# Gated cross-attention block: order of the tiled runs, place of the turned maxima and order of ScalarE's work in the attention steps

## The reference, cut to what matters

```
x (16, 100, 512), ctx (16, 361, 512), 16 query heads, 4 key heads, head size 32
Q = layernorm(x) @ Wq ; K = ctx @ Wk ; V = ctx @ Wv            # per batch entry
scores = Q K^T / sqrt(32) + slope * (key - query), masked
w = softmax(scores) ; out = (w V) @ Wo ; x = x + tanh(g0) * out
h = silu(q(ln(x)) q(Wg)) * (q(ln(x)) q(Wu)) ; h = rms_norm(h) ; x = x + tanh(g1) * q(h) q(Wd)
```

## Time and profile before

| what | value |
|---|---|
| median of three runs | 549.12 us |
| profiled execution, its span | 552.41 us, 550.6 us |
| TensorE busy | 485.2 us, 88% |
| VectorE busy | 363.5 us, 66% |
| ScalarE busy | 335.2 us, 61% |
| GpSimd busy | 236.8 us, 43% |
| chain that ended last, by engine | PE 66%, DVE 10%, DMA 9%, ACT 8%, issue 5% |

### The profile page before, as it was taken

How to read it: one execution, slowest core, us unless ns; L and a number is a source line. 1 busy time by engine, 2 the same in 40 slices (tenths; PEclk the granted TensorE clock), 3 DMA queues, 4 the chain that set the end, 5 groups by cost and what they waited for, 6 DMA issues and landing times.

```text
span 550.6 us, 8360 instructions
## 1 busy us (share of the span) xinstructions
PE 485.2 (88%) x2881; PEld 304.3 (55%) x2898; DVE 363.5 (66%) x672; ACT 335.2 (61%) x565; POOL 236.8 (43%) x253
## 2 busy tenths in 40 slices
PE   0699979997989989997999998589999999999964
PEld 0699979997944444443444444245455555555421
DVE  3786644386456777784988874166777777777750
ACT  0466646484246666765656676447777777777661
POOL 1000000000066767574264720066667676776650
PEclk9999989999989999998999999879999999999997
DMA  7879896999258897786676702002333333333222
GB/s 179 264 216 412 321 376 206 292 333 270 90 125 201 189 188 202 164 219 147 126 172 161 195 2 98 0 1 39 77 79 76 76 76 76 76 78 76 68 58 48
DMA packets 55666, 83.28 MB, mean 151 GB/s; under 512 B 30770, under 2 KB 42242, under 8 KB 53710
## 3 DMA queue, kind: packets, MB, share of 16 engines
q1 hardware_dynamic: 50446, 57.64, 40.9%
q0 software_dynamic: 3456, 12.58, 8.6%
q10 hardware_dynamic: 1728, 12.58, 6.5%
HBM read 57.29 MB, written 9.85 MB: 122 GB/s over the span
## 4 chain that ended last, share of the span: by engine, by line
PE 66%; DVE 10%; DMA 9%; ACT 8%; issue 5%; SPq 1%; POOL 0%; POOLq 0%; ACTq 0%; DVEq 0%
PE wide L1302 12%; PE bank L1136 10%; PE bank L1177 7%; PE bank L1312 7%; PE bank L1229 7%; PE bank L1219 6%; PE wide L1205 6%; PE bank L1232 5%; PE wide L1136 5%; DMA ct<-ctx_t 4%; ACT p_t L679 3%; DVE row_max L935 3%; DMA qs<-nm_t 2%; DMA wq_f<-wq 2%; ACT xq_f L718 1%
## 5 line engine op out<-in xcount | busy, mean ns | idle before, releaser
L935 DVE TENSOR_REDUCE row_max<-wide 100x2 f32<-100x722 f32 x128 | 110.4, 902 | 38.8 <-PE wide L1205 38.7
L679 ACT ACTIVATE p_t<-bank 121x400 f32<-121x400 f32 x192 | 92.5, 504 | 52.7 <-PE bank L1219 49.0
L1302 PE MATMUL wide<-w_q,xq 128*128 128x512 bf16 (+1 forms) x403 | 94.1, 384 | 1.6 <-ACT xq L726 0.8
L543 POOL TENSOR_TENSOR z<-h,lnw 128x512 f32<-128x512 f32 (+1 forms) x52 | 66.6, 1281 | 34.3 <-DVE h L1044 26.6
L1302 PEld LDWEIGHTS wide<-w_q,xq 128*128 128x128 bf16 (+1 forms) x416 | 40.1, 100 | 51.7 <-issue 6.6
L1312 PE MATMUL bank<-w_q,yq 128*128 128x512 bf16 (+1 forms) x204 | 51.0, 394 | 9.7 <-DMA yq<-y_int 9.2
L499 POOL DMA_DIRECT2D quant_in<-w_ffn x24 | 14.3, 597 | 101.3 <-PE bank L1177 94.8
L1205 PE MATMUL wide<-ks,qs 101*100 101x362 f32 x192 | 49.6, 346 | 9.4 <-DVE row_max L935 5.2
L774 ACT ACTIVATE act<-wide,small 128x512 f32<-128x512 f32 (+1 forms) x52 | 35.1, 680 | 35.3 <-PE wide L1302 23.4
L1219 PE MATMUL bank<-qs,ks 103*121 103x400 f32 x144 | 50.6, 381 | 6.4 <-DMA qs<-nm_t 3.1
L1177 PE MATMUL bank<-wv_f,ct 128*121 128x128 f32 x384 | 48.7, 288 | 3.3 <-DMA ct<-ctx_t 3.3
(11 more groups left out here) (139 smaller groups left out, 913.3 us busy)
## 6 DMA issues: line engine op xcount, KB each, us to landing
quant_in<-w_ffn POOLq DMA_DIRECT2D x24, 512.0 KB, 6.0
ct<-ctx_t SPq DMA_DIRECT2D x16, 722.0 KB, 9.9
ks<-k_all SPq DMA_DIRECT2D x36, 181.0 KB
q_scratch<-qhl SPq DMA_DIRECT2D x16, 400.0 KB, 8.1
abs_a<-w_ffn ACTq DMA_DIRECT2D x6, 1024.0 KB, 7.3
abs_b<-w_ffn ACTq DMA_DIRECT2D x6, 1024.0 KB, 8.9
qs<-q_scratch SPq DMA_DIRECT2D x12, 400.0 KB
xb<-x SPq DMA_DIRECT2D x12, 256.0 KB, 2.8
```

What stands on the lines that cost most here:

```text
L543: nc.gpsimd.tensor_tensor(z[par][0:rows, c], h[0:rows, c], lnw[0:rows, c], ALU.mult).then_inc(z_done, 1)
L679: nc.scalar.activation(p_t[:, j, :], bank[j % 2][0:KT, 0:HQ], ACT.Exp).then_inc(exp_done, 1)
L935: nc.vector.tensor_reduce(row_max[b % 2][:, 2 * u:2 * u + 2], wide[u % 2][0:SQ, :, 0:SK], AX_X, ALU.max).then_inc(s_maxed, 1)
L1302: mm = nc.tensor.matmul(wide[j % 2][0:rows, m, :], xq[:, c, 0:rows], w_q[:, m * C + c, 512 * j:512 * j + 512], start=(c == 0), stop=(c == ...
```

## The change

The table of what stands behind each pair of scores is new, so that PV0 and PV1 follow each other without anything between them. The transposed maxima go to columns 400 to 499 of bank 3 from entry 1 on. ScalarE does `turned_max` and e6, e7 before `log_sums` and `inverse_sums` of the older entry, and `keep_pv` after e'1 where it was after e'2. The wait of `scores(b, 1)` for `nm_ready` stays for b = 1 alone; PV0 waits for `nm_ready` instead, and the transposition waits for the copies of the step before.

```diff
-BEHIND = {0: [("t", 2, 4), ("t", 2, 5), ("pv", 2, 0), ("turn", 1, 0), ("t", 2, 6), ("t", 2, 7)],
-          1: [("t", 2, 8)],
-          2: [("t", 2, 9), ("t", 2, 10)],
-          3: [("t", 2, 11), ("pv", 2, 1)],
-          4: [("t", 1, 0)],
-          5: [("t", 1, 1), ("t", 1, 2), ("pv", 2, 2)],
-          6: [("t", 1, 3)],
-          7: []}
+BEHIND = {0: [("t", 2, 4), ("t", 2, 5), ("turn", 1, 0)],
+          1: [("t", 2, 6), ("t", 2, 7)],
+          2: [("t", 2, 8), ("t", 2, 9)],
+          3: [("pv", 2, 0), ("pv", 2, 1)],
+          4: [("t", 2, 10), ("t", 2, 11)],
+          5: [("t", 1, 0), ("t", 1, 1)],
+          6: [("pv", 2, 2), ("t", 1, 2)],
+          7: [("t", 1, 3)]}
...
+        def turned(b):
+            return wide[1][0:2 * H, 0, 400:400 + SQ] if b == 0 else bank[3][0:2 * H, 400:400 + SQ]
...
-                copy_high(nm_t[:, :], wide[1][0:2 * H, 0, 400:400 + SQ]).then_inc(nm_ready, 1)
+                copy_high(nm_t[:, :], turned(b)).then_inc(nm_ready, 1)
...
             def attention_step(b):
                 if b >= 2:
                     exps(b - 2, 4, 5)
-                if b >= 3:
+                if 2 <= b <= B:
+                    turned_max(b - 1)
+                if b == B + 1:
                     log_sums(b - 3)
                     inverse_sums(b - 3)
-                if 2 <= b <= B:
-                    turned_max(b - 1)
                 if b == B + 1:
                     xq_round(0)
                 if b >= 2:
                     exps(b - 2, 6, 7)
                 if b == B + 1:
                     xq_out(0)
+                if 3 <= b <= B:
+                    log_sums(b - 3)
+                    inverse_sums(b - 3)
                 if b >= 2:
                     exps(b - 2, 8, 9, 10, 11)
                 if b <= B:
-                    exps(b - 1, 0, 1, 2)
+                    exps(b - 1, 0, 1)
                 if b >= 2:
                     keep_pv(b - 2)
                 if b <= B:
-                    exps(b - 1, 3)
+                    exps(b - 1, 2, 3)
...
-                if b > 0 and u == 1:
-                    pe.wait_ge(nm_ready, b)
+                if b == 1 and u == 1:
+                    pe.wait_ge(nm_ready, 1)
...
+                if kt == 0:
+                    pe.wait_ge(nm_ready, min(b + 2, B))
...
             def turn_maxima(b):
                 pe.wait_ge(nm_split, b * 2 + 2)
-                nc.tensor.transpose(wide[1][0:2 * H, 0, 400:400 + SQ], nm_q[:, :].bitcast(F32), ident[0:SQ, 0:SQ]).then_inc(nm_turned, 1)
+                if b >= 2:
+                    pe.wait_ge(o_copied, (b - 1) * 2)
+                nc.tensor.transpose(turned(b), nm_q[:, :].bitcast(F32), ident[0:SQ, 0:SQ]).then_inc(nm_turned, 1)
```

## The result

Four runs of the changed kernel gave 565.91 us in the median (561.28 to 568.23), against 550.10 us for the kernel before (four runs, 547.73 to 552.56). The ratio is 1.0255, with an interval of 1.0201 to 1.031: 2.6% slower. The forecast was 551.6, in a range of 546.0 to 556.5, so the time lies outside it. The profiled execution took 568.23 us with a span of 566.4 us, 15.8 more than the one before.

A forecast was written before the change was run, and what follows sets the result against it. A woven chain, mostly on TensorE with short waits, was taken to bound the 11.65 us step. Terms -3.2 - 1.2 + 1.55 + 1.1 + 1.1 + 1.4 + 0.3 + 1.4 = +2.45 took 549.1 to 551.6 us, range 546.0 to 556.5.

The forecast's parts named there:

- The step itself: Undisturbed attention step, laid out from old distances: 11.42 us against 11.65, so -3.2 over fourteen steps.
- Step 9: t'0 waits for the stored maxima behind wo_f's load, issued 2.3 later in its step: +1.55.
- Step 16: The output product of 2.77 stands ahead of t6 and starves ScalarE: +1.4.
- The two new waits: PV0 waits for the maxima's copy, the transposition for keep_pv: both said to cost nothing.
- Step 2: PV run escapes the clock's lower level, as ScalarE paces that stretch: -1.2, or +1.4 if the clock is still low.
- VectorE has split the maxima by 1.13: In the laid-out step, row_max 7 and two operations of 0.2 end at 1.13, the transposition follows at 1.22.
- VectorE is later nowhere: Scores 6, at 8.58 in the laid-out step, need row_max 4, done at 8.08.
- In an undisturbed step I cost this at nothing: Stored maxima queued behind the later load on SyncE's queue: cover nearly gone, yet no cost in undisturbed steps.
- a cover between +0.25 and -0.85: Maxima wanted by t'0 at 8.15 in the step, forecast to land at 7.9 to 9.0.
- The first rival: Stored maxima wait behind the load in every step: +4.0 on the forecast, 555.6 us; chance 0.22.
- the forecast's own 2.65: DMA terms for late maxima: +1.55 in step 9 and +1.1 in steps 3 and 4.
- two one-off terms: wo_h holds ScalarE 1.90 before the fourth exponential: +1.1; wo_l holds VectorE 2.20 before row_max 0: +1.4.

The follow-up runs named there:

- e1: Changed kernel with the load of queries and keys cut to some 1/30 of the bytes from entry 4 on: 565.04 us, ratio 1.0273.
- e12: Changed kernel with the maxima's transposition behind t7, their store on ScalarE's queue, and wo_f's load and splits three steps later: 562.09 us.
- e13: Changed kernel with loads of the weights GpSimd quantises cut to 16 columns from the third block on, its operations whole: 561.64 us, ratio 1.0174.
- e7: Changed kernel with GpSimd's weight operations cut to 16 columns and the small load of queries and keys: 552.32 us, ratio 1.0007.
- e6: Kernel before the change with GpSimd's weight operations cut to 16 columns: 564.87 us, ratio 1.0259.
- e10: Changed kernel with the maxima's store issued by ScalarE on its own queue from entry 2 on: 589.17 us, ratio 1.0719.
- e4: Changed kernel with t10 and t11 ahead of the merged run, and ScalarE's logarithm and inverse behind four exponentials: 565.25 us, ratio 1.0315.

## Why the prediction was wrong

**Right.** The step itself, 11.43 where 11.42 was laid out, with the handovers of the earlier trace rows. Step 9: t'0 waited 3.86 where 2.73 + 1.55 was laid out. Step 16 and what follows: +2.3 where +1.4 stood, the same way though larger. The two new waits for banks (PV0 for the copy, the transposition for `keep_pv`) cost nothing, as said.

**Right in number only.** Step 2: scores 0 to scores 6 took 10.0 (157.04 to 167.07) against 11.6, so -1.6 where -1.2 stood. But an undisturbed step of the new order takes 8.7 for it (291.10 to 299.83), where the old one took 10.0, so step 2 is still 1.3 over its own order, with the granted clock at 0.50 until 162.7, where it was 1.6 over. The relief is 0.3; the rest comes of the new order reaching scores 6 earlier in every step. That the number fitted was luck.

**The first failed step** is "The two new waits cost nothing", in its last part: "VectorE has split the maxima by 1.13" and "VectorE is later nowhere". That left the transposition, at 1.22, a cover of 0.09. Before, a whole run of tiled matmuls stood between the earlier trace rows. I took the split's two operations as 0.2 each from an undisturbed step, and never asked what they last when GpSimd is at its weights, though the earlier trace rows show it there. Held, one of its operations takes 0.4 to 1.05 here and up to 1.3 in e1. Scores 1 and t6 stand behind the transposition in TensorE's order, so the wait holds them too. The sum had no term for this; it measured 5.0 in three steps.

**The second** is "In an undisturbed step I cost this at nothing", said of a cover between +0.25 and -0.85. An expected loss whose bounds reach to -0.85 in each of fourteen steps is not nothing. The first rival was this mechanism, and the alternation is its two-step loop. Its price of 4.0 on top of the forecast's own 2.65 is 6.65; 5.4 was measured. Its reason (the store cannot pass the load on one queue) is not enough after e12 and e13: it is the traffic of load and weights together.

**The third** is the size of two one-off terms. `wo_h` and `wo_l` stood at +1.1 and +1.4 over the kernel before. In e7, where nothing else is in the way, the two steps cost 8.1 us over undisturbed ones, against 1.1 in e6; in the changed kernel it is 8.0 against 1.2, with one held split in it: 6.8 where 2.5 stood. The waits were foreseen, the slower matmuls behind them were not.

With these three the account closes: for the thirteen steps the forecast had -3.0 + 2.65 + 2.5 = +2.15; 2.75 more for landings, 5.0 for held splits and 4.3 for `wo_f`'s splits make 14.2, and 14.1 was measured.

**Behind all three** stands an absent term: the clock. Working out -1.2 in step 2 I used the fall of the earlier trace rows, but costed no wait elsewhere at what it does to TensorE. Rows of the chain in the changed kernel, the merged run of step 11, behind a wait of 1.87 for VectorE that `wo_l` makes:

```profile
281.64 1.49 PE bank L1238 x8
...
283.12 1.33 PE bank L1241 x8
...
284.46 1.30 PE bank L1238 x8
...
285.75 0.67 PE bank L1241 x8
```

From 281.64 to scores 4 at 286.43 it takes 4.79 instead of 2.88, 1.9 more. From scores 4 to scores 4 this step took 16.07 (270.36 to 286.43), 4.6 over an undisturbed one. Four other runs on the chain are longer in the same way: at 180.90 by 1.1, at 256.67 by 1.3 (the kernel before has a fall of the clock there too, at 253 us), at 266.56 by 0.9, at 331.72 by 2.5. With step 11 that is 7.7 us, a lower bound, since other matmuls slow down too; 26 more microseconds at half the rate can cost at most 13. The Trainium skill (TensorE: Matmul & The Clock Gate, Part 1: The HAM clock gate) ties the clock to how busy TensorE has recently been; the falls behind the waits agree (at 254.9 at the end of the wait of 3.86, at 330.0 behind the one of 0.75). No experiment moved the clock alone, so how the 13.6 divide between waiting and the clock behind it stays open. The steps divide it by what starts it: the late landing, the held split and `wo_f`'s splits.

## What to carry to other kernels

A new order must be judged by the cover that it leaves to what it touches, not by its undisturbed step: here 0.23 us a step were gained and the cover of two handovers fell to about zero, one by an operation that another engine can hold for a whole microsecond, one by a transfer whose landing varies by several. Take each short operation on a tight path at its worst length in the whole trace, not in the one good step. And price a wait of TensorE with the slower matmuls that may come behind it: a wait of 0.75 us cost its step 3.9 here, and those of 1.27 and 1.85 in e7 cost 3.2 and 4.9.

## What the runs showed of the hardware

- GpSimd's operations on 128x1024 hold VectorE's of 16 columns until they end: 0.17 us becomes up to 1.3 (e1) or 1.5 (e13), with one SBUF input (L949) as with two (e10, 201.62). The held ones end 0.02 to 0.04 after GpSimd's.
- Relief of one disturbance raised the other: with quick loads (e1) the split waits went from four to eleven.
- The granted clock fell to 0.50 behind single idles of 0.75 to 3.9 us, though not behind each (not behind 1.08 at 323.23), and stayed there for some 3 to 7 us, in which eight tiled matmuls took 1.33 us instead of 0.67.
- A store of 32x100 values took 1.7 us to land where little else was under way and up to 9.0 with `wo_f`, the load and the weights on the DMA engines, whatever queue issued it (up to 7.1 on ScalarE's).
